# Conditioned attention on one core: scores before maxima in each step, the turn moved into a fill, and the last batch's rows loaded and biased one by one

## The chip, the cores and the metric

The kernel runs on one core of one Trainium2 chip. The metric is device time in microseconds (us) of one execution; three executions of the kernel before gave 1501.45, 1503.67 and 1509.83, median 1503.67.

## The reference, cut to what matters

Input x is [4, 1024, 512] (B batches, N tokens, D wide), 16 heads of 32. Everything is float32.

```python
h = _sln(x, w, ...)                      # layer norm, then gamma * ln + beta per batch
qkv = (h @ Wqkv.T + bqkv)                # q, k, v of 16 heads
energy = einsum('bhqd,bhkd->bhqk', q, k)
att = softmax(energy, axis=-1) / D ** 0.5
out = einsum('bhqk,bhkd->bhqd', att, v)
h1 = out @ Wp.T + bp + x
return _sln(h1, w, ...) + h1
```

There are 64 (batch, head) pairs. For each, the scores are a 1024 x 1024 matrix that is never stored: it is computed twice, once as A (rows are queries) to find each query's maximum, and once turned, as S^T (rows are keys), to be exponentiated and multiplied with v.

## The kernel before, in words

**Precision.** Projections split each float32 operand in a high and a low part and sum three products (`SPLIT`). A and S^T do the same in one matmul each, with parts stacked on partitions: A uses 96 rows (`a_item`, L737); S^T uses 98 rows (`turned_scores`, L751), the two more holding the negated maximum of each query in a high and a low part, so that S^T comes out with its maximum already subtracted.

**The clock of the program.** After a lead-in that projects five pairs of 128-token tiles, there are 16 iterations (i = 0 to 15) of four heads (s = 0 to 3), each head of eight steps (k = 0 to 7): step = 8 s + k. Each engine runs its own list of the same steps, and semaphores couple them. In every step TensorE (PE) does, in this order:

1. `project("start")`;
2. the first A block of the step (128 queries x 512 keys) into one of the two banks of `ps_a`;
3. the first S^T block of the next k (128 keys x 512 queries) into one of the three banks of `ps_st`;
4. `project("mid")`;
5. the second A block and, at k = 4, the turn (below);
6. the second S^T block;
7. in odd steps only, one set of pair sums (L781, 4 matmuls of 256 columns in four column groups, twice: softmax denominators) and 32 such matmuls in two calls of `weighted` (L768: v times the exponentials);
8. `project("end")`.

`project` takes a *fill*: a bank's worth of projection work. The table `PROJECTED` says which fill, which part and how many sixths of it run at which step and place. Fills 0 and 1 turn the normalised tiles (L691, four transposes each, at the start of steps 0 and 1); 2 to 5 are q and k (L702, matmuls of 256 columns); 6 and 7 are v and 8 and 9 the output projection (L649, matmuls of 512). Fills 0 to 7 belong to a later pair of tiles and are there in iterations 0 to 10 (`tiles`); 8 and 9 are there from iteration 4 on (`outs`). Every even step of iterations 4 to 9 has some 1.4 us of fill, half in the middle and half at the end (k = 2, 6) or all at the end (k = 0, 4). Iterations 11 to 14 have fills in steps 24 to 31 only; so in their first three heads the even steps hold nothing but A, S^T, A, S^T.

**Who releases whom.** VectorE (DVE) reduces each A block to a maximum per query (L1223, `half_max`); an A block may start when the reduction of the block two before it is done (`a_used`, two banks). A head's 16 blocks are spread so that the last is in step k = 3 of the head before; `max_negated` (L1240) then joins the halves. At k = 4, PE *turns* the 128 x 8 maxima into a row form: item 16, L731, a transpose that also takes a bank of `ps_a`, so that three items share that step's ring. DVE splits the result (`ring_row`, L1230 and L1232), SyncE (SP) copies it at k = 5 into rows 96 and 97 of `q_stack` (`store_row`, L435), and the next head's S^T, first needed at k = 7, waits for that copy (`row_in`).

ScalarE (ACT) exponentiates each S^T block (L999) into `p32`; an S^T block may start when the exponential of the block three before it is done. GpSimd (POOL) adds pairs of exponential slabs (`pair_add`, L1495) at k = 0, 2, 4, 6, and PE's pair sums wait for that: at k = 7 for the pair added at k = 4, and so on. POOL also has the layer norms (`norm_scale`, `norm_gain`, iterations 0 to 9), `residual`, `out_norm`, `out_low`, and the output's `out_scale` and `out_finish` (L1400 to L1414), which sit at steps 29, 31 and steps 1, 3 of the next iteration. `out_scale` at step 29 waits for statistics that DVE takes in step 28, behind `ring_row` on that engine.

**The last batch's rows.** The last batch's output is finished in another way: eight row tiles `acc[0..7]` hold x plus the bias `bp`, and the attention output is added to them at the end. `load_acc` (L480) on SP, after iteration 11's list, issues eight loads of 256 KB, all on one semaphore; `acc_add` (L1416) on POOL, also after iteration 11's list, waits for all eight and adds the bias to each (L1419). Their first reader is `pre_sum` in iteration 15. acc[0] to acc[3] lie in `x_tile` and `h_tile`, acc[4] to acc[7] in `qkT_s`, which are free once iteration 10 has projected its last tile.

Of the kernel before, what the change touches and what calls it, by code (L numbers as in the profile page):

```python
# [32 lines left out]
for _fill in range(3, 10):  # L33
    PROJECTED[4 * _fill - 8, "end"] = [(_fill, 0, 0, 6)]
    PROJECTED[4 * _fill - 6, "mid"] = [(_fill, 1, 0, 3)]
    PROJECTED[4 * _fill - 6, "end"] = [(_fill, 1, 3, 6)]
EVACUATED = {0: 0, 1: 1, 2: 3, 3: 7, 4: 11, 5: 15, 6: 19, 7: 23, 8: 27, 9: 31}
# [22 lines left out]
def conditioned_attention(nc, x, cond, ln_g, ln_b, Wg, bg, Wb, bb, Wqkv, bqkv, Wp, bp, out):  # L60
# [33 lines left out]
    with ExitStack() as ctx:  # L94
# [126 lines left out]
        acc_in = sem("acc_in")  # L221
# [29 lines left out]
        PRE_ADD_STEP = {17 + 2 * t: t for t in range(8)}  # L251
        LATE_MM_STEP = {8: 0, 10: 1}
# [100 lines left out]
        def _(sp):  # L353
# [126 lines left out]
            def load_acc():  # L480

                sp.wait_ge(tile_mm, 8 * PAIRS)
                for t in range(8):
                    T = 2 * END + t
                    sp.dma_start(acc[t], x_rows[T * 128:(T + 1) * 128, :]).then_inc(acc_in, 16)

# [65 lines left out]
            def iteration(i, tiles, norms, outs, first=False, last=False):  # L552
                pair = i - FIRST_OUTS
                for s in range(4):
                    u = 4 * i + s
                    for k in range(8):
# [34 lines left out]
                        if last and step == 5:  # L591

                            sp.wait_ge(out_pool, 10 * pair + ONE)
                            load_gain(go_s, go_in, pair)
                        if last and step in PRE_LOAD_STEP:
# [23 lines left out]
            iteration(LAST_TILES, False, False, True)  # L619
            load_acc()  # L620
# [21 lines left out]
        def _(pe):  # L642
# [193 lines left out]
            def iteration(i, tiles, outs, first=False, last=False):  # L836
                pair = i - FIRST_OUTS
                for s in range(4):
                    for k in range(8):
# [25 lines left out]
                        for use in uses[:1]:  # L865
                            a_item(*use)
# [3 lines left out]
                        if after:  # L870
                            turned_scores(*after, 0)
                        project("mid")
                        for use in uses[1:]:
                            a_item(*use)
                        if after:
                            turned_scores(*after, 1)
                        before = (i - (s == 0), (s - 1) % 4)
# [17 lines left out]
                        project("end")  # L895

# [435 lines left out]
        def _(pool):  # L1332
# [83 lines left out]
            def acc_add(t):  # L1416

                pool.wait_ge(acc_in, 128)
# [99 lines left out]
            def iteration(i, tiles, norms, outs, first=False, late=True):  # L1518
                pair = i - FIRST_OUTS
                ahead = i + LEAD  # L1520
                for step in range(32):
# [11 lines left out]
                    if norms and step in NORM_GAIN_STEP:  # L1533
                        norm_gain(ahead + 1, NORM_GAIN_STEP[step])
                    if outs and step in RESIDUAL_STEP:
# [19 lines left out]
            iteration(LAST_TILES, False, False, True)  # L1555
            for t in range(8):
                acc_add(t)
# [31 lines left out]
```

## Time and profile before

| | us |
|---|---|
| three executions | 1501.45, 1503.67, 1509.83 |
| median | 1503.67 |
| profiled execution, its own time | 1507.32 |
| its span | 1504.9 |
| PE busy | 1388.0 (92%) |
| POOL busy | 1004.3 (67%) |
| DVE busy | 916.5 (61%) |
| ACT busy | 715.4 (48%) |
| mean granted PE clock | 0.973 |

Engines are busy in the sense that an instruction of theirs is under way; successive matmuls overlap, so how fast PE goes is read from the distance between the starts of successive matmuls, not from its busy share. A wait stands in square brackets behind the instruction that ended it, with what released it.

### The profile page before, as it was taken

Reading aid. Unit: us, or ns where it says so; the run is one execution under the profiler, and the core shown is the slowest. Engines: PE = TensorE matmul, PEld = TensorE weight load, DVE = VectorE, ACT = ScalarE, POOL = GpSimd, SP = SyncE. Lnnn points to the kernel's source line nnn. Section 1 sums busy time; section 2 is a strip of 40 time slices with the busy share of each in tenths; the row PEclk is TensorE's granted clock in tenths of the full one; section 3 lists DMA queues with packets and bytes.
Section 4 is the critical chain, followed back from the end, with each engine's and each line's share of the span. In section 5 each row is a group of like instructions: output and inputs, shape, how many; then the busy total and the mean of one; then the engine's idle time right before and its main releaser. Section 6 shows DMA issues by size and latency. Waiting matters only on the chain.

```text
span 1504.9 us, 35271 instructions
## 1 busy us (share of the span) xinstructions
PE 1388.0 (92%) x10884; PEld 905.4 (60%) x10884; DVE 916.5 (61%) x1634; ACT 715.4 (48%) x1371; POOL 1004.3 (67%) x763
## 2 busy tenths in 40 slices
PE   6898999999999999999999999999996999998994
PEld 4887666666565657666666666666553454544562
DVE  5335766666666666666666666665663665665625
ACT  4221555555555555455454555455552545554441
POOL 2442455556465778687787878676877877787945
PEclk8899999999999999999999999999997998999997
DMA  7567533323334544445354534335333323243221
GB/s 226 154 188 207 135 88 109 98 88 98 103 99 120 135 110 130 99 140 135 105 146 121 147 101 130 97 114 137 87 103 106 106 82 101 77 116 95 67 65 59
DMA packets 216697, 174.01 MB, mean 116 GB/s; under 512 B 105492, under 2 KB 186516, under 8 KB 216632
## 3 DMA queue, kind: packets, MB, share of 16 engines
q1 hardware_dynamic: 214456, 166.83, 41.2%
q0 software_dynamic: 1984, 6.29, 1.1%
q8 instruction: 35, 0.57, 0.2%
q14 instruction: 30, 0.25, 0.1%
q10 hardware_dynamic: 192, 0.07, 0.0%
HBM read 113.29 MB, written 58.51 MB: 114 GB/s over the span
## 4 chain that ended last, share of the span: by engine, by line
PE 65%; POOL 14%; issue 9%; DVE 5%; POOLq 2%; DMA 1%; ACT 1%; SPq 1%; DVEq 0%; ACTq 0%
PE ps_a L737 13%; PE ps_st L751 11%; PE ps_o L768 11%; PE ps_w L702 8%; PE ps_w L649 7%; POOL p L1495 7%; PE ps_s L781 7%; DVE half_max L1223 3%; PE ps_st L702 3%; POOLq L1355 1%; POOL y_t L1412 1%; POOL y_t L1410 1%; PE ps_w L815 1%; PE ps_a L731 1%; PE ps_s L702 1%
## 5 line engine op out<-in xcount | busy, mean ns | idle before, releaser
L1223 DVE TENSOR_REDUCE half_max<-ps_a 128x1 f32<-128x512 f32 x1024 | 670.1, 687 | 455.8 <-PE ps_a L737 454.4
L999 ACT ACTIVATE p<-ps_st 128x512 f32<-128x512 f32 x1024 | 572.4, 597 | 490.2 <-PE ps_st L751 455.2
L1495 POOL TENSOR_TENSOR p<-p 128x1024 f32<-128x1024 f32 x248 | 590.7, 2384 | 300.1 <-PE ps_o L768 299.0
L737 PE MATMUL ps_a<-k_stack,q_stack 96*128 96x512 f32 x1024 | 449.4, 441 | 11.5 <-DVE half_max L1223 7.1
L751 PE MATMUL ps_st<-q_stack,k_stack 98*128 98x512 f32 x1024 | 415.1, 407 | 14.1 <-ACT p L999 14.1
L737 PEld LDWEIGHTS ps_a<-k_stack,q_stack 96*128 96x128 f32 x1024 | 193.9, 190 | 181.4 <-issue 99.1
L768 PE MATMUL ps_o<-p,v_head 128*32 128x256 f32 x4096 | 272.6, 384 | 0.0
L751 PEld LDWEIGHTS ps_st<-q_stack,k_stack 98*128 98x128 f32 x1024 | 195.4, 191 | 46.3 <-ACT p L999 25.2
L768 PEld LDWEIGHTS ps_o<-p,v_head 128*32 128x32 f32 x4096 | 134.4, 111 | 91.7 <-issue 6.3
L781 PE MATMUL ps_s<-p,root_s 128*32 128x256 f32 x1984 | 160.9, 397 | 20.1 <-POOL p L1495 18.5
L702 PEld LDWEIGHTS ps_w<-hT_s,wqkv_s 128*128 128x128 f32 x1056 | 143.7, 189 | 9.8
L702 PE MATMUL ps_w<-hT_s,wqkv_s 128*128 128x256 f32 x1056 | 146.6, 283 | 0.0
L781 PEld LDWEIGHTS ps_s<-p,root_s 128*32 128x32 f32 x1984 | 39.2, 108 | 110.5 <-issue 83.4
L649 PE MATMUL ps_w<-wqkv_s,hT_s 128*128 128x512 f32 x324 | 87.2, 395 | 0.0
L649 PE MATMUL ps_w<-wp_s,oT_s 128*128 128x512 f32 x288 | 78.3, 396 | 1.3 <-DVE h_t L1158 1.3
L649 PEld LDWEIGHTS ps_w<-wqkv_s,hT_s 128*128 128x128 f32 x324 | 60.9, 189 | 13.5
L649 PEld LDWEIGHTS ps_w<-wp_s,oT_s 128*128 128x128 f32 x288 | 53.7, 189 | 13.9 <-issue 1.7
L702 PE MATMUL ps_st<-hT_s,wqkv_s 128*128 128x256 f32 x360 | 49.9, 299 | 7.8 <-DVE hT_s L1122 7.8
L702 PEld LDWEIGHTS ps_st<-hT_s,wqkv_s 128*128 128x128 f32 x360 | 48.5, 205 | 9.6 <-DVE hT_s L1122 9.1
L1353 POOL TENSOR_TENSOR std_t<-mv_t,eps_s 128x1 f32<-128x1 f32 x32 | 6.0, 189 | 70.2 <-DVE mv_t L1082 70.2
L974 ACT ACTIVATE o_stage<-ps_o 128x256 f32<-128x256 f32 x63 | 24.2, 384 | 56.2 <-PE ps_o L768 56.2
L1373 POOL TENSOR_TENSOR h_tile<-h_tile,gq_s 128x512 f32<-128x512 f32 x32 | 41.1, 1283 | 14.7 <-DMA gq_s<-gain_bias_scratch 13.5
(167 smaller groups left out, 1003.8 us busy)
## 6 DMA issues: line engine op xcount, KB each, us to landing
qk_scratch<-qkT_s SPq DMA_DIRECT2D x108, 256.0 KB, 2.4
q_stack<-qk_scratch SPq DMA_DIRECT2D x192, 128.0 KB, 2.8
k_stack<-qk_scratch SPq DMA_DIRECT2D x192, 128.0 KB, 3.0
x_tile<-in_x SPq DMA_DIRECT2D x34, 256.0 KB, 5.1
gq_s<-gain_bias_scratch SPq DMA_DIRECT2D x16, 512.0 KB, 4.2
v_scratch<-v_parts SPq DMA_DIRECT2D x32, 256.0 KB, 3.3
v_head<-v_scratch SPq DMA_DIRECT2D x64, 128.0 KB, 2.1
att_scratch<-o_stage SPq DMA_DIRECT2D x240, 32.0 KB, 1.5
```

Of the source, the lines that this page charges most:

```text
L649: mm = pe.matmul(dst, left[:, lp, c, :], right[:, rp, c, :], start=(n == 0), stop=(n == 11))
L702: mm = pe.matmul(bank[:, part * 256:(part + 1) * 256], wqkv_s[:, lp, w, d, chunk * 128:(chunk + 1) * 128], hT_s[:, rp, d, :], start=(n == ...
L731: pe.transpose(ps_a[0:8, parity, 0:128], neg_max[:, s % 2, :], f_ident).then_inc(a_ready, 1)
L737: pe.matmul(ps_a[:, parity, :], q_stack[0:96, s, t * 128:(t + 1) * 128], k_stack[0:96, s, half * 512:(half + 1) * 512], start=True, stop=T ...
L751: pe.matmul(ps_st[:, ST_BANK[2 * k + e], :], k_stack[0:98, s, k * 128:(k + 1) * 128], q_stack[0:98, s, e * 512:(e + 1) * 512], start=True, ...
L768: mm = pe.matmul(ps_o[HD * e:HD * e + HD, 0:QW], v_head[:, s, k, :], p32[:, k, e * QW:(e + 1) * QW], start=(k == 0), stop=(k == 7))
L781: mm = pe.matmul(ps_s[HD * e:HD * e + HD, 0:QW], root_s[:], p32[:, 2 * j + 1, e * QW:(e + 1) * QW], start=(j == 0), stop=(j == 3))
L974: nc.scalar.activation(o_stage[:, s % 2, 0:QW], ps_o[:, 0:QW], ACT.Copy).then_inc(o_taken, 1)
L999: nc.scalar.activation(p32[:, k, e * 512:(e + 1) * 512], ps_st[:, ST_BANK[2 * k + e], :], ACT.Exp).then_inc(exp_done, 1)
L1223: V.tensor_reduce(half_max[:, s % 2, item:item + 1], ps_a[:, parity, :], AX.X, ALU.max).then_inc(a_used, 1)
L1373: G.tensor_tensor(h, h, gq_s[:, 0, :], ALU.mult).then_inc(ln_pool, 1)
L1495: G.tensor_tensor(p32[:, 2 * j + 1, :], p32[:, 2 * j, :], p32[:, 2 * j + 1, :], ALU.add).then_inc(pair_added, 1)
```

## The change

In each step PE issues S^T, A, S^T, A where it issued A, S^T, A, S^T. The place of `project("start")` and of the odd steps' sums and weighted products is the same.

The turn (the third item at k = 4) moves from between the second A and the second S^T to the end of the step. The fill parts that stood at the end of steps 4, 12, 20 and 28 are cut in two halves, and the turn is issued between the halves. In the last iteration it follows the second A directly.

`load_acc` and `acc_add` are issued one tile at a time inside iteration 11 (`gather=True`), at the steps of two new tables, with two semaphores for four tiles each in place of one for eight.

```diff
+for _step in (4, 12, 20, 28):
+    _fill = _step // 4 + 2
+    PROJECTED[_step, "end"] = [(_fill, 0, 0, 3)]
+    PROJECTED[_step, "last"] = [(_fill, 0, 3, 6)]
...
-        acc_in = sem("acc_in")
+        acc_in = [sem(f"acc_in{e}") for e in range(2)]
...
+        ACC_LOAD_STEP = {2: 0, 3: 1, 5: 2, 6: 3, 12: 4, 15: 5, 16: 6, 18: 7}
+        ACC_ADD_STEP = {9: 0, 10: 1, 11: 2, 13: 3, 22: 4, 24: 5, 25: 6, 27: 7}
...
-            def load_acc():
-
-                sp.wait_ge(tile_mm, 8 * PAIRS)
-                for t in range(8):
-                    T = 2 * END + t
-                    sp.dma_start(acc[t], x_rows[T * 128:(T + 1) * 128, :]).then_inc(acc_in, 16)
+            def load_acc(t):
+
+                if t == 0:
+                    sp.wait_ge(tile_mm, 8 * PAIRS)
+                T = 2 * END + t
+                sp.dma_start(acc[t], x_rows[T * 128:(T + 1) * 128, :]).then_inc(acc_in[t // 4], 16)
...
+                        if gather and step in ACC_LOAD_STEP:
+                            load_acc(ACC_LOAD_STEP[step])
...
-            iteration(LAST_TILES, False, False, True)
-            load_acc()
+            iteration(LAST_TILES, False, False, True, gather=True)
...
                         project("start")
-                        for use in uses[:1]:
-                            a_item(*use)
                         after = (i, s, k + 1) if k < 7 else (i + (s + 1) // 4, (s + 1) % 4, 0)
                         if last and (s, k) == (3, 7):
                             after = None
                         if after:
                             turned_scores(*after, 0)
+                        for use in uses[:1]:
+                            a_item(*use)
                         project("mid")
-                        for use in uses[1:]:
-                            a_item(*use)
                         if after:
                             turned_scores(*after, 1)
+                        for use in uses[1:2]:
+                            a_item(*use)
+                        if last:
+                            for use in uses[2:]:
+                                a_item(*use)
...
                         project("end")
+                        if not last:
+                            for use in uses[2:]:
+                                a_item(*use)
+                        project("last")
...
-                pool.wait_ge(acc_in, 128)
+                pool.wait_ge(acc_in[t // 4], 64)
                 G.tensor_tensor(acc[t], acc[t], bp_s[:], ALU.add).then_inc(acc_ready, 1)
...
+                    if gather and step in ACC_ADD_STEP:
+                        acc_add(ACC_ADD_STEP[step])
...
-            iteration(LAST_TILES, False, False, True)
-            for t in range(8):
-                acc_add(t)
+            iteration(LAST_TILES, False, False, True, gather=True)
```

## Rows read from the trace of the kernel before

**Rows 1.** The page, part 4: the chain that ended last, by engine

```profile
PE 65%; POOL 14%; issue 9%; DVE 5%; POOLq 2%; DMA 1%; ACT 1%; SPq 1%; DVEq 0%; ACTq 0%
```

**Rows 2.** Five iterations: length; busy us of PE, PEld, DVE, ACT, POOL; clock; DMA; GB/s

```profile
644.10:728.80 84.70, 81.99 (x670) 55.25 (x670) 55.20 (x100) 43.73 (x85) 65.95 (x51) 1.00 0.46 124
...
1065.70:1137.20 71.50, 67.74 (x542) 36.81 (x541) 47.42 (x84) 39.37 (x74) 57.73 (x39) 1.00 0.36 99
1137.20:1225.00 87.80, 71.47 (x542) 38.36 (x541) 47.51 (x84) 39.31 (x74) 67.20 (x47) 0.88 0.36 100
1225.00:1301.70 76.70, 71.42 (x541) 38.53 (x540) 47.50 (x84) 39.36 (x74) 57.38 (x39) 0.93 0.34 90
1301.70:1373.90 72.20, 67.68 (x541) 36.80 (x540) 47.38 (x84) 39.43 (x74) 57.51 (x39) 1.00 0.35 96
```

**Rows 3.** Timeline of PE: an even step with fill, no turn

```profile
707.57 0.50 PE L737 MATMUL ps_a<-k_stack,q_stack 96*128 96x512 f32 x1
...
710.02 0.39 PE L737 MATMUL ps_a<-k_stack,q_stack 96*128 96x512 f32 x1
```

**Rows 4.** Timeline of PE: step 28 of i = 6, fill and turn

```profile
717.38 0.50 PE L737 MATMUL ps_a<-k_stack,q_stack 96*128 96x512 f32 x1
...
718.74 0.27 PE L731 MATMUL ps_a<-ident,neg_max 128*8 128x128 f32 x1 [0.41 <-DVE half_max L1223]
...
719.19 1.55 PE L649 MATMUL ps_w<-wp_s,oT_s 128*128 128x512 f32 x6
720.59 0.39 PE L737 MATMUL ps_a<-k_stack,q_stack 96*128 96x512 f32 x1
```

**Rows 5.** Timeline of PE: a turn in i = 10, which is no loop

```profile
995.41 0.27 PE L731 MATMUL ps_a<-ident,neg_max 128*8 128x128 f32 x1 [0.31 <-DVE half_max L1223]
995.44 0.48 PE L751 MATMUL ps_st<-q_stack,k_stack 98*128 98x512 f32 x1
```

**Rows 6.** Timeline of PE: steps 0 and 1 of i = 7

```profile
728.04 0.65 PE L691 MATMUL ps_w<-ident,h_tile 128*128 128x128 f32 x4
...
729.86 0.50 PE L751 MATMUL ps_st<-q_stack,k_stack 98*128 98x512 f32 x1 [0.49 <-ACT p L999]
...
732.28 0.50 PE L751 MATMUL ps_st<-q_stack,k_stack 98*128 98x512 f32 x1 [0.44 <-ACT p L999]
732.71 0.64 PE L781 MATMUL ps_s<-p,root_s 128*32 128x256 f32 x8
```

**Rows 7.** Timeline of ACT, the same steps

```profile
729.22 1.08 ACT L999 ACTIVATE p<-ps_st 128x512 f32<-128x512 f32 x2
```

**Rows 8.** Timeline of DVE, the end of step 31 and step 0

```profile
727.12 0.68 DVE L1158 TENSOR_TENSOR h_t<-ps_w,res_t 128x512 f32<-128x512 f32 x1
...
729.71 0.68 DVE L1122 TENSOR_TENSOR hT_s<-ps_w,hT_s 128x512 fp32r<-128x512 f32 x1
```

**Rows 9.** Timeline of PE: an even and an odd step of i = 11, no fill

```profile
1095.97 0.50 PE L737 MATMUL ps_a<-k_stack,q_stack 96*128 96x512 f32 x1
...
1097.26 0.49 PE L737 MATMUL ps_a<-k_stack,q_stack 96*128 96x512 f32 x1
...
1098.52 0.64 PE L781 MATMUL ps_s<-p,root_s 128*32 128x256 f32 x8
```

**Rows 10.** Timeline of SP: the row copies of that head

```profile
1093.79 1.43 SPq L435 DMA_DIRECT2D q_stack<-max_rows  x2
```

**Rows 11.** Timelines of POOL and PE: the last batch's rows

```profile
1145.65 2.47 POOL L1419 TENSOR_TENSOR x_tile<-x_tile,bp_s 128x512 f32<-128x512 f32 x2 [6.42 <-DMA qkT_s<-in_x]
...
1157.78 1.08 PE L781 MATMUL ps_s<-p,root_s 128*32 128x256 f32 x8 [13.65 <-POOL p L1495]
```

**Rows 12.** PE waits for POOL at step 7 of i = 13, 14; then a stretch

```profile
1242.89 1.08 PE L781 MATMUL ps_s<-p,root_s 128*32 128x256 f32 x8 [2.24 <-POOL p L1495]
...
1318.74 0.64 PE L781 MATMUL ps_s<-p,root_s 128*32 128x256 f32 x8 [1.50 <-POOL p L1495]
...
1243.00:1255.00 12.00, 11.91 (x72) 5.83 (x76) 5.48 (x9) 5.67 (x11) 6.88 (x3) 0.63 0.21 50
```

More of the change, by code:

```diff
@@ L550, in _, with iteration @@
                 store_v(LEAD - 1, a)
-            def iteration(i, tiles, norms, outs, first=False, last=False):
+            def iteration(i, tiles, norms, outs, first=False, last=False, gather=False):
                 pair = i - FIRST_OUTS
@@ L1516, in finish_late, with iteration @@
                     out_finish(pair, 1, count)
-            def iteration(i, tiles, norms, outs, first=False, late=True):
+            def iteration(i, tiles, norms, outs, first=False, late=True, gather=False):
                 pair = i - FIRST_OUTS
```

## The prediction

> **What bounds the kernel now.** I read the chain first, then the iterations one by one, then the timelines of PE inside a step. The chain [rows 1] is PE for 65% and POOL for 14%, so PE's pace decides except where POOL holds it. The iterations [rows 2] say where: i = 6, with all its fills, takes 84.7 us; i = 11 and i = 14, with few, take 71.5 and 72.2; i = 12, with the work of i = 14, takes 87.8, and i = 13 takes 76.7. Both of these have a granted clock under 1. In a full iteration PE's starts follow each other with hardly a hole; what is lost there are small waits that come back in each iteration, and these a new order can touch. A half per cent (7.5 us) is about what a measurement of this kernel can tell from no change.
>
> **1. The last batch's rows.** POOL stands 6.42 us for the eight loads and then has eight additions of about 1.25 us (2.47 for two) in one piece; PE waits 13.65 us for a pair sum behind them and then runs at the low clock for a while [rows 11]. With the additions spread, i = 12 has the same lists as i = 14 on every engine. I take its length: 87.8 - 72.2 = 15.6 us gained; by i = 13 it would be 11.1 [rows 2]. The additions, 10 us, go into i = 11, where POOL is idle for 71.5 - 57.7 = 13.8 us [rows 2]; a pair addition may be some 4 us late before PE's sums ask for it, and no step gets more than one of 1.25 us. So I cost them at nothing; without that cover it would be at most 10. On SP the eight loads are issued between its other transfers, two at most in neighbouring steps of 1.3 to 2.7 us; a transfer holds SP's queue for some 0.7 us (1.43 for two, [rows 10]), and behind them wait stack loads for a head three ahead. The first addition is at step 9, three steps after the fourth load. Nothing.
>
> **2. The turn.** An even step with six fill matmuls and no turn takes 710.02 - 707.57 = 2.45 us from its first A to the next [rows 3]; with a turn 720.59 - 717.38 = 3.21 [rows 4]. So a turn costs 0.76 us, and 0.41 of that is a wait: it is the third item in a ring of two, and the reduction of the step's first A is not done. After three fill matmuls (half of the 1.4 us between 719.19 and 720.59) that reduction is done with about 0.2 us to spare, and the bank is handed back before the second A of the next step. What remains of the cost is the turn itself and perhaps a weight load behind it that nothing hides. From below it is 0.03, the distance from a turn to the next matmul in [rows 5]; from above, 0.35, all of the 0.76 but the wait. I take 0.15, near the low end, since the distance is of the same instruction and the rest of the 0.76 is what follows a stall. Gain 0.6 in a loop; in i = 0 and 10, which are no loops, the wait is 0.31 [rows 5] and I take 0.45. Turns with a fill that PE's own pace bounds: 3 in each of i = 0 to 3, 4 in i = 4 to 9, 3 in i = 10: 39, of which 6 in i = 0 and 10. 33 x 0.6 + 6 x 0.45 = 22.5 us.
>
> The rows show weight loads of 0.19 us hidden in a stream whose matmuls start every 0.23 us. The Trainium skill (TensorE: Matmul & The Clock Gate, "The mechanism" in Part 3) says that a weight load overlaps running matmuls only where its row group differs. By that rule the turn and the fill behind it would each pay their load, and the saving would be nearer 0.4 a turn, some 15 us in all. The stream of loads over the same rows speaks against it here; I stay with 22.5.
>
> **3. The new order where fills are.** Exchanging A with S^T changes no count, and the waits it could touch are few. In steps 0 and 1 of i = 0 to 10 it costs. The second S^T of step 0 starts at 729.86 because an exponential ends there that had to follow the copy of the fill turned at 728.04 [rows 6, 7]; the new order doesn't move that, but one A (0.33 behind a stall) now comes after it in place of before. In step 0 most of this is hidden, since the next transposes wait for VectorE's subtraction that ends at 730.4 [rows 8]; that one is 0.1 later, as the first A is. In step 1 the sums at 732.71 [rows 6] come 0.34 later. 11 x 0.34 = +3.7 us. In step 31, VectorE's sum of h1 [rows 8] follows the second reduction, which is 0.23 later, and the transposes of step 0 follow it: +0.2 at six starts of iterations, +1.2.
>
> **4. The new order where no fill is.** From the first A to the sums of the next step: 1098.52 - 1095.97 = 2.55 us, with the third A at 1.29, when the first one's reduction is done [rows 9]. Now S^T goes first (0.34), the third A is at 0.34 + 1.19 = 1.53, the fourth, by two reductions of 0.65, at 2.14, and the sums at 2.47 to 2.57. So each of some 45 such pairs of steps gains 0.08 or loses 0.02; 12 of the turns there are where the turn has no fill to stand in, worth up to 0.1 each to the bad. I take -1 for all, bounds -3.6 and +2. The row copy is later relative to its reader here: it is issued at 1093.79 for 1.43 us [rows 10], and the reader comes some 2.3 us after that ends; the change takes 0.7 of it. Nothing, but little is left: a copy that lands 1 us late would be waited for.
>
> **5. POOL at the start of iterations.** From step 29 to step 7 POOL is behind: PE waits 2.24 and 1.50 us at step 7 of i = 13 and 14 [rows 12]. This run of work begins with statistics that VectorE takes behind the turn, and the turn of step 28 is now 0.36 later in its step. So at the five starts of i = 11 to 15 the turn's saving (not counted above) is lost and 0.36 added: +1.8 us. PE's wait there grows by 0.9. After 2.24 us of it the clock was 0.63 over 12 us, so about 9 us at the low of its levels, 1.2 in place of 2.4 GHz, 4.5 us lost; after 1.50 it was not [rows 12, 2]. With waits of 2 to 3 us, i = 11, 12 and 14 can fall too. I put this at +3.5, between 0 and three times 4.5.
>
> **The sum.** -15.6 - 22.5 + 3.7 + 1.2 - 1 + 1.8 + 3.5 = -28.9 us. The profiled execution took 1507.3 (span 1504.9) and would take 1478.4. It stands 3.6 above the median of the runs; from the median, 1503.7, it is **1474.8 us**.
>
> **The rivals.**
> - *Only the rows gain (chance 0.09).* PE gets ahead by each turn and hands it back in a wait for ScalarE or POOL. For: the waits of 0.49 and 0.44 [rows 6] show that S^T can be held. Against: in a full iteration POOL is busy 66 of 84.7 us and ScalarE 44 [rows 2]. Time: 1503.7 - 15.6 = 1488.
> - *The clock falls at every start without fills (0.05).* i = 11, 12, 14 and 15 each lose 4.5 as i = 13 does: 1474.8 - 3.5 + 18 = 1489.
> - *The stall of i = 12 moves into i = 11 (0.03).* Its POOL is late at steps 9 to 13 or 22 to 27 by the whole 10 us, and PE waits for it: 1485.
> - *A dearer border (0.03, slower).* In every odd step S^T now follows the weighted products and the sums follow A; no row shows either. S^T after A starts at 0.23, but behind a drained array at 0.34. If each of the two borders in 256 odd steps costs that difference of 0.11, it is 56 us: 1531. From 0.056 a border (29 us) it decides. Against: both loads take 0.19, and A and S^T follow fills alike.
> - *Nothing changes (0.01)*: the turn still waits in its new place, and a wait elsewhere takes the rest.
>
> **The numbers.** The forecast has 0.79. Its own bounds: turns at 0.8 of their saving or 1.1, clock from 0 to 9, rows 11.1 or 15.6, no-fill steps from -3.6 to +2: about 1465 to 1486. For 8 in 10 with the other cases I take 1464 to 1491. Faster by over 0.5% (under 1496.2) 0.94, within 0.03, slower 0.03.
>
> **What would show it.** Right: no wait of PE before the turn in iterations 0 to 10, and a full iteration of about 83 us in place of 84.7 (4 x 0.6 less 0.34 and 0.2); i = 12 between 72 and 77; POOL's L1419 in eight single pieces with no wait for loads; the wait before the sums of step 7 longer than 2 us in i = 13. Wrong: a full iteration of 84.7, with new waits of L751 for ACT; turns that still wait for DVE; L1419 followed by a wait of L781 in i = 11; distances over 0.34 at the borders of odd steps.

## The result and the profile after

The changed kernel takes 1481.96 us (median of 4, 1479.04 to 1484.65) against 1502.82 (median of 4, 1501.45 to 1509.83). The ratio is 0.9852, with a 95% interval of 0.9815 to 0.9888: 20.9 us less, where 28.9 were forecast; it lies inside the range. The two profiled executions stand 28.3 us apart (1507.32 and 1479.04), close to the forecast, but that is luck: the one before is among the longer of its kernel, the one after is the shortest of its own. What differs between executions of one kernel comes up below.

The chain that ended last has moved little against [rows 1]: PE has 67% of it where it had 65%, DVE 3% where it had 5%.

```profile
PE 67%; POOL 14%; issue 9%; DVE 3%; POOLq 2%; DMA 2%; ACT 1%; SPq 1%; ACTq 0%; DVEq 0%
```

By iterations, with the columns of [rows 2]: i = 6, 8, 11, 12, 13 and 14.

```profile
634.90:718.90 84.00, 82.33 (x670) 55.57 (x669) 55.49 (x100) 43.10 (x84) 65.90 (x51) 0.98 0.47 125
801.40:883.90 82.50, 80.82 (x672) 55.22 (x670) 55.53 (x100) 43.00 (x84) 65.87 (x51) 1.00 0.48 129
1049.50:1122.50 73.00, 67.54 (x545) 37.61 (x541) 47.42 (x84) 38.64 (x74) 67.03 (x47) 1.00 0.46 124
1122.50:1196.90 74.40, 69.12 (x544) 38.36 (x540) 47.39 (x84) 38.79 (x74) 57.47 (x39) 0.98 0.35 92
1196.90:1271.20 74.30, 68.97 (x544) 38.53 (x540) 47.50 (x84) 38.88 (x74) 57.46 (x39) 0.98 0.35 93
1271.20:1344.20 73.00, 67.54 (x545) 37.66 (x541) 47.43 (x84) 38.76 (x74) 57.48 (x39) 1.00 0.35 95
```

A full iteration such as i = 8 went from 84.6 to 82.5. Iteration 12 went from 87.8 to 74.4, but 11 and 14, at 73.0, are longer than before (71.5 and 72.2). And i = 6 has 1.5 us more than i = 8 with the same work, at a clock of 0.98: that is new against the trace of the kernel before, where all iterations up to 11 had a clock of 1.00 (traces of other kernels in the old order have some too, as counted below).

The turn of step 28 of i = 6 (timeline of PE), which answers to [rows 4]:

```profile
708.27 0.50 PE L758 MATMUL ps_st<-q_stack,k_stack 98*128 98x512 f32 x1
...
709.31 0.87 PE L656 MATMUL ps_w<-wp_s,oT_s 128*128 128x512 f32 x3
710.02 0.27 PE L738 MATMUL ps_a<-ident,neg_max 128*8 128x128 f32 x1
710.04 0.94 PE L656 MATMUL ps_w<-wp_s,oT_s 128*128 128x512 f32 x3
710.83 0.40 PE L758 MATMUL ps_st<-q_stack,k_stack 98*128 98x512 f32 x1
```

It waits for nothing, and the step takes 710.83 - 708.27 = 2.56 us, 0.11 more than the 2.45 of the same step without a turn [rows 3] and 0.65 less than before. The weight loads of the same place (timeline of PEld) lie over running matmuls: the turn's own, 0.08 us, begins at 709.87, and the next one of the fill at 710.02.

```profile
709.87 0.08 PEld L738 LDWEIGHTS ps_a<-ident,neg_max 128*8 128x8 f32 x1
710.02 0.53 PEld L656 LDWEIGHTS ps_w<-wp_s,oT_s 128*128 128x128 f32 x3
```

The start of i = 8, steps 0 and 1, which answers to [rows 6]:

```profile
801.00 0.65 PE L698 MATMUL ps_w<-ident,h_tile 128*128 128x128 f32 x4 [0.27 <-DVE h_t L1172]
...
802.83 0.50 PE L758 MATMUL ps_st<-q_stack,k_stack 98*128 98x512 f32 x1 [0.70 <-ACT p L1013]
803.16 0.39 PE L744 MATMUL ps_a<-k_stack,q_stack 96*128 96x512 f32 x1
...
805.34 0.51 PE L758 MATMUL ps_st<-q_stack,k_stack 98*128 98x512 f32 x1 [0.71 <-ACT p L1013]
805.68 0.40 PE L744 MATMUL ps_a<-k_stack,q_stack 96*128 96x512 f32 x1
806.01 0.64 PE L788 MATMUL ps_s<-p,root_s 128*32 128x256 f32 x8
```

From the transposes to the sums it is 5.01 us where it was 4.67: the waits of S^T for ACT are 0.70 and 0.71 where they were 0.49 and 0.44, with an A behind each, and the transposes now wait 0.27 for the sum of h1.

The last batch's rows (timeline of POOL, i = 11) are biased in single pieces with no wait for their loads; PE's wait of 13.65 us [rows 11] is gone.

```profile
1072.20 1.27 POOL L1433 TENSOR_TENSOR x_tile<-x_tile,bp_s 128x512 f32<-128x512 f32 x1
1073.44 2.38 POOL L1509 TENSOR_TENSOR p<-p 128x1024 f32<-128x1024 f32 x1
```

At step 7 of i = 12, PE waits 2.24 us for POOL and goes on at the low clock; L775 takes 1.95 where it takes 1.05 at full clock. The same wait is 1.86 in i = 11, 2.25 in i = 13 and 2.26 in i = 14; after those of i = 11 and 14 the clock stayed at 1.00. The lines of i = 12:

```profile
1140.71 0.85 PE L788 MATMUL ps_s<-p,root_s 128*32 128x256 f32 x8 [2.24 <-POOL p L1509]
1141.32 1.95 PE L775 MATMUL ps_o<-p,v_head 128*32 128x256 f32 x16
```

### The profile page after: what moved, and what is told of

Read it like the earlier page. It is cut to its first block, busy times and chain, and to the rows that moved or that the text cites. A ratio compares the mean times of both kernels' runs of the same rounds, so it can differ in the third digit from the quotient of the medians.

```text
span 1476.4 us, 35271 instructions
## 1 busy us (share of the span) xinstructions
PE 1376.7 (93%) x10884; PEld 910.2 (62%) x10884; DVE 920.9 (62%) x1634; ACT 706.4 (48%) x1371; POOL 1004.0 (68%) x763
## 4 chain that ended last, share of the span: by engine, by line
PE 67%; POOL 14%; issue 9%; DVE 3%; POOLq 2%; DMA 2%; ACT 1%; SPq 1%; ACTq 0%; DVEq 0%
PE ps_st L758 14%; PE ps_a L744 12%; PE ps_o L775 11%; PE ps_w L709 9%; POOL p L1509 8%; PE ps_w L656 8%; PE ps_s L788 7%; PE ps_st L709 3%; DVE half_max L1237 2%; POOLq L1369 1%; POOL y_t L1426 1%; POOL y_t L1424 1%; PE ps_w L822 1%; ACT p L1013 1%; PE ps_w L698 1%
## 5 line engine op out<-in xcount | busy, mean ns | idle before, releaser
L1013 ACT ACTIVATE p<-ps_st 128x512 f32<-128x512 f32 x1024 | 565.4, 597 | 419.4 <-PE ps_st L758 392.7
L758 PE MATMUL ps_st<-q_stack,k_stack 98*128 98x512 f32 x1024 | 439.4, 431 | 22.4 <-ACT p L1013 22.0
L744 PE MATMUL ps_a<-k_stack,q_stack 96*128 96x512 f32 x1024 | 421.2, 413 | 12.7 <-DVE half_max L1237 8.5
L775 PE MATMUL ps_o<-p,v_head 128*32 128x256 f32 x4096 | 272.7, 385 | 0.0
L775 PEld LDWEIGHTS ps_o<-p,v_head 128*32 128x32 f32 x4096 | 134.3, 111 | 91.2 <-issue 4.6
L788 PE MATMUL ps_s<-p,root_s 128*32 128x256 f32 x1984 | 160.5, 395 | 11.4 <-POOL p L1509 9.7
L709 PE MATMUL ps_w<-hT_s,wqkv_s 128*128 128x256 f32 x1056 | 149.9, 286 | 0.0
```

Of the source, the lines that this page charges most:

```text
L709: mm = pe.matmul(bank[:, part * 256:(part + 1) * 256], wqkv_s[:, lp, w, d, chunk * 128:(chunk + 1) * 128], hT_s[:, rp, d, :], start=(n == ...
L744: pe.matmul(ps_a[:, parity, :], q_stack[0:96, s, t * 128:(t + 1) * 128], k_stack[0:96, s, half * 512:(half + 1) * 512], start=True, stop=T ...
L758: pe.matmul(ps_st[:, ST_BANK[2 * k + e], :], k_stack[0:98, s, k * 128:(k + 1) * 128], q_stack[0:98, s, e * 512:(e + 1) * 512], start=True, ...
L775: mm = pe.matmul(ps_o[HD * e:HD * e + HD, 0:QW], v_head[:, s, k, :], p32[:, k, e * QW:(e + 1) * QW], start=(k == 0), stop=(k == 7))
L788: mm = pe.matmul(ps_s[HD * e:HD * e + HD, 0:QW], root_s[:], p32[:, 2 * j + 1, e * QW:(e + 1) * QW], start=(j == 0), stop=(j == 3))
L1013: nc.scalar.activation(p32[:, k, e * 512:(e + 1) * 512], ps_st[:, ST_BANK[2 * k + e], :], ACT.Exp).then_inc(exp_done, 1)
```

## The experiments

The theory was the sum of the prediction with its parts independent: rows, turn, order, POOL's start, clock. The main rival was that the order belongs to the turn's gain. The question that the result added was what the missing 8 us were. The kernel before was measured again beside each group of runs, and its medians there lie between 1502.8 and 1505.3; so medians of different groups compare to some 2.5 us only, and the ratios, each to the kernel before beside it, are the safer figures.

### The parts one by one

**e1: rows alone.** Edit, on the kernel before: the hunks of `load_acc`, `acc_add` and their tables, nothing else.

```diff
-            iteration(LAST_TILES, False, False, True)
-            for t in range(8):
-                acc_add(t)
+            iteration(LAST_TILES, False, False, True, gather=True)
```

> The kernel before with only the last batch's rows loaded and biased one by one in iteration 11. Theory (the three parts add up; the rows part is worth what iteration 12 lost): iteration 12 falls from 87.8 us to 72 to 77, iteration 11 stays at 71.5, and the time is 1487 to 1491 against 1503. Rival (additions in iteration 11 delay POOL, as the wait at step 5 of iteration 11 in the changed kernel might say): iteration 11 is longer by 1 us or more here too, and the time is over 1492.

Measured: 1491.35 us, ratio 0.9916 (0.9897 to 0.9935), 11.9 less than the 1503.22 of the kernel before beside it. Iterations 11, 12 and 13:

```profile
1056.20:1130.60 74.40, 69.06 (x541) 37.20 (x540) 47.45 (x84) 39.27 (x74) 67.53 (x47) 0.98 0.43 122
1130.60:1202.80 72.20, 67.74 (x541) 36.86 (x541) 47.41 (x84) 39.42 (x74) 57.67 (x39) 1.00 0.34 96
1202.80:1276.20 73.40, 68.95 (x541) 37.66 (x541) 47.46 (x84) 39.51 (x74) 57.58 (x39) 0.98 0.35 94
```

Iteration 12 has the 72.2 us that it was to have, 15.6 less. But i = 11 has 2.9 more at a clock of 0.98. PE at steps 5 and 7 of i = 11 (timeline of PE), where the kernel before had a single wait of 1.11 at step 7 and no low clock after it:

```profile
1077.31 0.64 PE L784 MATMUL ps_s<-p,root_s 128*32 128x256 f32 x8 [0.80 <-POOL p L1498]
...
1083.25 1.08 PE L784 MATMUL ps_s<-p,root_s 128*32 128x256 f32 x8 [1.89 <-POOL p L1498]
```

POOL's additions begin only at step 9, so it isn't they that hold POOL. It is late from its start: its third instruction of the output's scale for the second tile comes after a gap of 1.86 us that no other engine ends, where the kernel before has 0.24. The timeline of POOL at that place, before and then e1:

```profile
1070.79 0.57 POOL L1356 TENSOR_TENSOR ostd_t<-ostd_t,minus_half 128x1 f32<-128x1 f32 x1 [0.24 <-issue]
```

```profile
1072.02 0.57 POOL L1359 TENSOR_TENSOR ostd_t<-ostd_t,minus_half 128x1 f32<-128x1 f32 x1 [1.86 <-issue]
```

The traces say what ends the gap: the landing of the output tile that POOL stored itself a little earlier. In the program a `pool.drain()` stands just before this instruction (`power`, L1355 in the kernel before). In e1 the store is issued at 1066.83 and takes 5.0 us to land, so it is there at 1071.84, and the instruction starts at 1072.02; before, it was issued at 1067.22 and took 2.9, so that it had landed at 1070.11 and nothing was left to wait for. The stores, before and then e1 (timeline of POOL, and the list of the DMAs issued at that moment, with their size and the us to landing):

```profile
1067.22 0.63 POOL L1414 DMA_DIRECT2D out_y<-y_t  x1 [0.29 <-POOL y_t L1412]
out_y<-y_t POOLq DMA_DIRECT2D x1, 256.0 KB, 2.9
```

```profile
1066.83 0.63 POOL L1417 DMA_DIRECT2D out_y<-y_t  x1 [0.29 <-POOL y_t L1415]
x_tile<-in_x SPq DMA_DIRECT2D x2, 256.0 KB, 4.9
out_y<-y_t POOLq DMA_DIRECT2D x1, 256.0 KB, 5.0
```

In all fourteen traces, wherever POOL stands over 0.3 us at this place (111 times), it goes on 0.18 us after its last store has landed, and nowhere does it go on sooner. In i = 11 the gap is 0.8 to 1.9 us in every trace with the row loads there (the changed kernel, e1, e4 to e8, e11, e12) but that of e9, whose POOL issues its store of the first tile earlier and has 0.24. Without the loads it is 0.24 (before, e2, e3) or 0.57 (e10). But the row loads aren't needed for it: in every trace but e9's it is 1.7 to 3.9 us in i = 5 to 9 and 1.0 to 2.0 in i = 15, and in i = 13 of the kernel before it is 1.18. That the row loads make the store of i = 11 land late is argued from this comparison; no run moved them alone.

So both theories had a part, and the time is 0.4 past the range of the first: the wait of i = 12 went, and the work moved into i = 11 isn't free there. 15.6 less in i = 12 and 2.9 more in i = 11 make 12.7, within the interval of the 11.9. The other differences of these two traces (1.5 more in i = 6, 3.3 less in i = 13) hold low clock that falls otherwise in each execution. The profiled execution of the kernel before was one of its longer ones; the one of e1 is near its median.

**e2: order alone.** S^T, A, S^T, A; the turn third, behind the second A; no fill cut.

```diff
-                        for use in uses[:1]:
-                            a_item(*use)
                         if after:
                             turned_scores(*after, 0)
+                        for use in uses[:1]:
+                            a_item(*use)
                         project("mid")
-                        for use in uses[1:]:
-                            a_item(*use)
                         if after:
                             turned_scores(*after, 1)
+                        for use in uses[1:]:
+                            a_item(*use)
```

> The kernel before with only S^T, A, S^T, A in each step; the turn stays the third item, behind the second A, with no fill cut. Theory (the order by itself only costs: 0.33 in steps 0 and 1 of eleven iterations, 0.23 in step 31 of six, 0.5 at step 20 of four, and stretches of low clock that begin at these waits): 1503 + 4 + 1.4 + 2 + 0 to 5 = 1510 to 1516. Rival (the order is what lets the turn go without a wait, so it gains with it): the turn's step is shorter here than 3.21 us by 0.2 or more, and the time is at most 1503.

Measured: 1515.88 us, ratio 1.007 (1.0053 to 1.0087), 12.7 more and inside the expected range. The order by itself only costs. Its turn waits as before, and the step is no shorter (3.30 us here, 3.21 in [rows 4]):

```profile
725.98 0.27 PE L731 MATMUL ps_a<-ident,neg_max 128*8 128x128 f32 x1 [0.41 <-DVE half_max L1223]
```

**e3: turn alone.** The turn between the halves of the end fill, order A, S^T, A, S^T.

```diff
-                        for use in uses[1:]:
+                        for use in uses[1:2] if not last else uses[1:]:
                             a_item(*use)
...
                         project("end")
+                        if not last:
+                            for use in uses[2:]:
+                                a_item(*use)
+                        project("last")
```

> The kernel before with only the turn moved into the middle of the end fills; order A, S^T, A, S^T kept. Theory (the turn's saving of 0.67 us in a loop and 0.49 outside needs no new order): 39 turns save 25 us, less 1 to 2 us at the starts of iterations 11 to 15: 1479 to 1482. Rival (part of the saving comes with the new order, which puts a matmul more between the first A and the turn): the turn still waits, and the time is over 1487.

Measured: 1484.01 us, ratio 0.9865 (0.9846 to 0.9884), 19.2 less. The turn waits for nothing and costs the same 0.1 us as in the changed kernel, so its gain needs no new order:

```profile
703.84 0.87 PE L653 MATMUL ps_w<-wp_s,oT_s 128*128 128x512 f32 x3
704.54 0.27 PE L735 MATMUL ps_a<-ident,neg_max 128*8 128x128 f32 x1
704.57 0.94 PE L653 MATMUL ps_w<-wp_s,oT_s 128*128 128x512 f32 x3
```

The 19.2 is 2 us past the end of what was expected: 39 turns are worth 25, and 6, not 1 to 2, are given back later (e7 and e8). Its trace says the same: 24.8 less than before in iterations 0 to 10, 5.5 more behind them.

**e4: turn and rows, the old order.** The changed kernel with the body of a step as in e3.

> The changed kernel with the old order A, S^T, A, S^T (turn inside the fill and rows one by one kept). Theory (the new order costs 3.6 + 1.4 us of waits at the starts of iterations, 2 us at step 20, and up to 5 us of low clock): 1470 to 1475, faster than the changed kernel's 1482 by 7 to 12, and no stretch at the low clock in iterations 1 to 10. Rival (the order is neutral and the stretches of low clock come by chance): 1479 to 1484, with such stretches here too.

Measured: 1470.57 us, ratio 0.978 (0.9757 to 0.9802): 11.4 less than the changed kernel's 1481.96 (the two intervals don't meet), and no stretch of low clock in iterations 1 to 10. The parts add up: 19.2 + 11.9 = 31.1 against 32.7 for both together, and the order takes 11.4 to 12.7 of that back. It does so in the early iterations: 1 to 10 take 817.9 and 816.1 us in the two traces of the changed kernel and 808.0 in e4, 11 to 14 take 294.7 and 299.5 against 298.6.

### What the order costs

**e5: the old order in steps 0 and 1 of iterations 0 to 10 only.**

```diff
+                        early = tiles and step < 2
+                        if early:
+                            for use in uses[:1]:
+                                a_item(*use)
                         if after:
                             turned_scores(*after, 0)
-                        for use in uses[:1]:
-                            a_item(*use)
+                        if not early:
+                            for use in uses[:1]:
+                                a_item(*use)
```

(and the same around the second pair).

> The changed kernel with the order A, S^T, A, S^T in steps 0 and 1 of iterations 0 to 10 alone. Theory (there the second S^T waits for an exponential behind the copy of a turned fill, and an A placed after it costs 0.33 us an iteration and leaves PE idle long enough for the clock to fall now and then): iterations 1 to 10 each 0.33 us shorter, no stretch at the low clock in them, 3.6 us less and up to 5 more: 1475 to 1479. Rival (the stretches are chance): 1478.5, and such stretches stay.

Measured: 1475.03 us, ratio 0.9802 (0.9786 to 0.9819): 6.9 less than the changed kernel, from twenty-two of its 512 steps (7.6 less than e6 below, which was measured beside it and takes what the changed kernel takes). A full iteration takes 82.1 where the changed kernel's i = 8 takes 82.5:

```profile
795.40:877.50 82.10, 80.79 (x669) 55.33 (x668) 55.28 (x100) 43.00 (x84) 65.78 (x50) 1.00 0.49 130
```

The waits themselves are 11 x 0.34 = 3.7 us of it. The rest fits the clock: no low stretch here in iterations 1 to 10, and by the count under e11 the new order has some 1.9 more of them in an execution, at 1.5 us each: 2.8.

**e6: ScalarE's copies one step later in iterations 11 to 14.** In these, step 21 had become longer, 3.33 us where it had been 2.66.

```diff
-                    highs = LATE_HIGH_STEP if last else OUT_HIGH_STEP
+                    highs = LATE_HIGH_STEP if last else OUT_HIGH_STEP if tiles else {20: 0, 22: 1}
```

> The changed kernel with ScalarE's two copies for the output projection (steps 19 and 21) one step later in iterations 11 to 14. Theory (S^T of step 20 waits there for an exponential behind such a copy, which itself waits for POOL's multiplication of step 18): steps 20 to 22 of iterations 11 to 14 shorter by 0.5 each, 2 us in all: 1480. Rival (the waits at steps 20 to 22 come from the ring of A and its reductions): no change, 1482, steps 21 still 3.3 us.

Measured: 1482.58 us, ratio 0.9848 (0.9827 to 0.9869). PE in i = 12 of the changed kernel, from S^T of step 20 that waits for ACT to the first S^T of steps 21 and 22:

```profile
1169.27 0.51 PE L758 MATMUL ps_st<-q_stack,k_stack 98*128 98x512 f32 x1 [0.38 <-ACT p L1013]
...
1169.89 0.49 PE L758 MATMUL ps_st<-q_stack,k_stack 98*128 98x512 f32 x1
...
1173.22 0.50 PE L758 MATMUL ps_st<-q_stack,k_stack 98*128 98x512 f32 x1
```

And with the copies later:

```profile
1174.31 0.49 PE L758 MATMUL ps_st<-q_stack,k_stack 98*128 98x512 f32 x1
...
1177.13 0.50 PE L758 MATMUL ps_st<-q_stack,k_stack 98*128 98x512 f32 x1
```

Step 21 is 2.82 in place of 3.33, so the wait was of these copies, and it is of the new order's making, which asks for that S^T 0.23 us earlier. The total is unchanged: the 2 us don't show beside low stretches that fell otherwise. As a gain this is not shown.

**e11: the changed kernel once more, for its trace.** No edit.

> The changed kernel unaltered, for one more trace. Theory (the new order's longer waits in steps 0 and 1 let the clock fall now and then): one to four stretches of about 3.3 us at the low clock at the starts of iterations 1 to 10, not at the same iterations as before, and all other step lengths the same to 0.03 us. Rival (they are of the program, not of chance): the same three places.

Measured: 1482.75 us (one run). Low stretches at the starts of i = 4 and 8, at 474 and 805 us; in the first trace they were at 393, 640 and 970. In iterations 11 to 14 the clock fell after the wait at step 7 in all four, where in the first trace it fell in 12 and 13 alone. The step lengths are the same elsewhere. This is how one looks, i = 6 of the first trace, step 1:

```profile
638.85 0.50 PE L758 MATMUL ps_st<-q_stack,k_stack 98*128 98x512 f32 x1 [0.70 <-ACT p L1013]
639.19 0.56 PE L744 MATMUL ps_a<-k_stack,q_stack 96*128 96x512 f32 x1
639.68 1.08 PE L788 MATMUL ps_s<-p,root_s 128*32 128x256 f32 x8
640.54 1.93 PE L775 MATMUL ps_o<-p,v_head 128*32 128x256 f32 x16
```

I counted such stretches (matmuls at twice their spacing for over 2 us) in iterations 1 to 10 of every trace. With the new order in steps 0 and 1 (the changed kernel twice, e2, e6): 9 in 40 iterations. With the old order there (the kernel before, e1, e3, e4, e5, e7 to e10, e12): 4 in 100. So they are tied to no iteration, and come some five times as often where PE stands 0.70 and 0.71 us in steps 0 and 1 as where it stands 0.49 and 0.44; a split as uneven as 9 and 4 would come once in some 600 times if the stretches fell on any iteration alike. A stretch of 3.2 us costs 1.5, as i = 6 beside i = 8 shows.

### POOL's start

**e7: the statistics of step 28 taken in step 27**, on e4.

```diff
-OUT_STATS_STEP = {28: 0, 31: 1}
+OUT_STATS_STEP = {27: 0, 31: 1}
```

> The faster version (turn inside the fill and rows one by one, old order) with VectorE's output statistics of step 28 taken in step 27, ahead of the turn's split. Theory (POOL's run of work at the starts of iterations 11 to 15 begins with these statistics, and PE's wait of 2.25 us at step 7 hangs on its start): PE's waits there fall to about 1 us and the clock stays up: iterations 11 to 14 at 71 to 73 us in place of 74.2 to 75.2, time 1462 to 1467 against 1470.6. Rival (POOL is late for another reason, the amount of its work between the steps): waits stay over 2 us, 1469 to 1472.

Measured: 1459.99 us, ratio 0.9694 (0.9678 to 0.9711): 10.6 less than e4 and 2 below the expected range (13 less if the ratios are compared). PE's wait at step 7 of i = 13, e4 first, then e7:

```profile
1203.97 0.64 PE L788 MATMUL ps_s<-p,root_s 128*32 128x256 f32 x8 [2.25 <-POOL p L1506]
```

```profile
1201.76 0.64 PE L788 MATMUL ps_s<-p,root_s 128*32 128x256 f32 x8 [1.22 <-POOL p L1506]
```

In i = 14 the same wait went from 2.27 to 1.25. Iteration 14 in e4 and in e7:

```profile
1260.80:1335.90 75.10, 70.24 (x544) 38.19 (x540) 47.51 (x84) 38.96 (x74) 57.46 (x39) 0.95 0.32 93
```

```profile
1256.20:1327.80 71.60, 67.80 (x545) 36.71 (x541) 47.37 (x84) 38.99 (x74) 57.56 (x39) 1.00 0.35 97
```

One microsecond less of wait and a clock of 1.00 in place of 0.95: 3.5 us in one iteration. The largest wait of this kind is at step 5 of i = 15, where ScalarE stands for POOL and PE for ScalarE: PE's was 3.52 us before the change, 4.84 in the changed kernel, 4.75 in e4, and is 2.77 here.

**e8: the turn of step 28 in its old place, in iterations 11 to 14 only**, on e4.

```diff
+                        soon = last or (step == 28 and not tiles)
-                        for use in uses[1:2] if not last else uses[1:]:
+                        for use in uses[1:] if soon else uses[1:2]:
                             a_item(*use)
...
-                        if not last:
+                        if not soon:
```

> The same faster version with the turn of step 28 of iterations 11 to 14 back in its old place between the second A and the second S^T. Theory (moving that turn gave POOL a start 0.36 us later and PE 0.67 us less, so it only lengthened PE's wait at step 7, past the length at which the clock falls): PE's wait falls from 2.25 to about 1.2 to 1.5 us, iterations 12 to 15 lose 0.3 to 2.5 us each, time 1463 to 1470. Rival (the turn saves its 0.67 us there as elsewhere): 4 x 0.67 us more, 1473.

Measured: 1465.37 us, ratio 0.9732 (0.9716 to 0.9748): 5.2 less than e4 (7 by the ratios) for undoing four of the turns. The wait at step 7 of i = 14 is

```profile
1278.30 0.64 PE L788 MATMUL ps_s<-p,root_s 128*32 128x256 f32 x8 [1.50 <-POOL p L1507]
```

that is, what it was before the change [rows 12]. Moving a turn to save PE 0.67 us cost 1.3 us net here, through POOL and the clock.

**e9: also `out_scale` at step 27 and `out_finish` at 29**, on e7.

```diff
-OUT_SCALE_STEP = {29: 0}
-OUT_FINISH_STEP = {31: 0}
+OUT_SCALE_STEP = {27: 0}
+OUT_FINISH_STEP = {29: 0}
```

> The faster version with the statistics in step 27, and also POOL's out_scale at step 27 in place of 29 and out_finish at 29 in place of 31. Theory (POOL's run of work at the starts of iterations 11 to 15 only starts too late; before step 29 POOL has some 6 us idle): PE's waits at step 7, 1.2 to 1.9 us with the statistics moved alone, go, and the time is 1453 to 1458 against 1460. Rival (the run is bound by its amount from step 31 on, where out_scale of the second tile still waits): waits of over 1 us stay, 1459 to 1461.

Measured: 1462.24 us, ratio 0.9709 (0.9687 to 0.9732): nothing gained over e7's 1459.99; the 2 us more are within the intervals. The waits at step 7 of i = 12 to 14 are 1.50 and 1.77, longer than e7's 0.89 to 1.25.

The edit doesn't do what the theory asks for. At the start of i = 13, POOL's scale of the first tile comes 1.2 us earlier than in e7, after a wait of 3.70 for the statistics; but a pair addition that went ahead of it in e7 comes behind it, and the scale of the second tile, which decides, begins 1.15 us later. So e9 says nothing against a late start. In i = 13 of the traces in the old order, PE's wait goes with the lateness of that second scale and the gap behind the store (both of POOL):

| | second scale, us after the start of i = 13 | gap | PE's wait at step 7 |
|---|---|---|---|
| e7 | 4.10 | 0.67 | 1.22 |
| e8 | 4.79 | 0.24 | 1.44 |
| e12 | 4.10 | 1.30 | 1.81 |
| e9 | 5.25 | 0.24 | 1.77 |
| e4 | 5.85 | 0.24 | 2.25 |

Each wait is the sum of the first two columns less 3.6 to 3.8 us. e7 and e12 start at the same moment there, and PE's wait differs by the 0.6 us by which the gap does. So a part of what e7 leaves is POOL standing for its own store; the rest, POOL's work from step 29 on, is argued.

**e10: the same statistics in step 27 in the kernel before.**

> The kernel before with the statistics of step 28 taken in step 27, nothing else. Theory (POOL's late start binds there too, by the waits of 1.1 to 2.2 us at step 7, but without the turn's saving it binds less): 3 to 8 us less than before, 1495 to 1500. Rival (before the change these waits were too short to matter and only the moved turn made them count): within 2 us of before, 1501 to 1505.

Measured: 1505.59 us, ratio 1.0002 (0.9989 to 1.0015): no change. Full iterations are 85.2 where they were 84.6 (the statistics hold DVE when the first A of step 28 comes, and the turn, still third in its ring, waits for that too), and i = 14 is 71.6:

```profile
733.10:818.40 85.30, 81.90 (x672) 55.21 (x670) 55.12 (x100) 43.65 (x84) 65.97 (x50) 1.00 0.47 124
1304.30:1375.90 71.60, 67.71 (x544) 36.79 (x540) 47.25 (x84) 39.37 (x74) 57.46 (x39) 1.00 0.37 97
```

The time is the rival's, 0.8 from the kernel before beside it, but not for the rival's reason: the waits at step 7 were there and went, from 1.11, 2.24 and 1.50 in i = 11, 13 and 14 to 0.25, 0.80 and 0.28. Six full iterations that are 0.6 longer, 3.6 us, took it back.

**e12: the statistics in step 27 only from iteration 10 on**, on e4.

```diff
+                        when = OUT_STATS_STEP if norms else {27: 0, 31: 1}
-                        if outs and step in OUT_STATS_STEP and not last:
-                            a = OUT_STATS_STEP[step]
+                        if outs and step in when and not last:
+                            a = when[step]
```

> The faster version with the statistics in step 27 only from iteration 10 on, and in step 28 in iterations 4 to 9 as in the kernel before. Theory (taken earlier, they hold VectorE when the first A of step 28 comes, and so cost PE 0.3 us in each full iteration, where POOL has time to spare; they gain only at the starts of iterations 11 to 15): iterations 4 to 9 back at 81.9 us, iterations 11 to 14 at 71 to 72, time 1457 to 1459. Rival (what is gained there is lost again in stretches of low clock): 1460 to 1462.

Measured: 1457.75 us, ratio 0.9686 (0.967 to 0.9702), the lowest median: 24.2 less than the changed kernel, 45.7 less than the kernel before beside it. It isn't told apart from e7's ratio of 0.9694, whose interval overlaps; that iterations 4 to 9 are back at 81.9 is what the trace shows. Iterations 8 and 14:

```profile
794.30:876.20 81.90, 80.81 (x672) 55.23 (x669) 55.31 (x100) 43.27 (x84) 65.89 (x51) 1.00 0.48 130
...
1254.80:1326.30 71.50, 67.70 (x544) 36.69 (x540) 47.32 (x84) 38.96 (x74) 57.54 (x39) 1.00 0.35 97
```

## Why the prediction was right, and where it was off

It was right that the kernel gets faster, by two of three parts, and that the new order is no gain. That the time came within 8 us owes something to terms that err against each other. The rows gave 3.7 less than forecast and the order cost 7.5 to 8.8 more; turn and POOL's start together gave 2.0 more than forecast (e3: 19.2 against 22.5 - 5.3), and the parts together 1.6 more than singly. That leaves 7.6 to 8.9 of the missing 8. By its own steps:

- **The rows, step 1: right in place, too large in size.** The 15.6 of i = 12 came in full, yet the rows alone gave -11.9 (e1). That POOL's additions cost nothing held: POOL is busy 67.0 of 73.0 us of i = 11, no addition waits and nothing waits for one. The term that failed is the nothing at which the loads were put: with them beside it POOL stands 0.8 to 1.9 us in place of 0.24 for the landing of its own store, PE waits longer behind it, and i = 11 takes 2.9 us more in e1. That the loads delay the store is argued from which traces have it; no run moved the loads alone.
- **The turn, step 2: right.** 0.11 us left of 0.76 where 0.15 was taken; 33 x 0.65 and 6 x 0.49 make 24.4 where the sum had 22.5. The rule of the Trainium skill (TensorE: Matmul & The Clock Gate, "The mechanism" in Part 3) that a weight load overlaps running matmuls only where its row group differs, by which a turn would have saved some 0.4, is not borne out: the turn's 0.02 to the next matmul and 0.08 more for the three after it leave no room for two weight loads of 0.08 and 0.19 laid end to end.
- **The order where fills are, step 3: the sizes right, a consequence missed.** 0.34 a start was forecast for steps 0 and 1 and 0.34 came, 0.2 for h1 and 0.23 came. What the step didn't price is that longer waits there make the clock fall: 9 in 40 starts against 4 in 100. Together with steps 20 to 22 it is this that failed: steps 3 and 4 summed to +3.9 and the order costs 11.4 to 12.7 (e2, e4). e5 puts 6.9 of that in steps 0 and 1 alone. With 1.4 for h1 and the 2.0 at steps 20 to 22, whose removal in e6 gained nothing, 10.3 of it has a name.
- **The order where no fill is, step 4: no gain.** An even and an odd step take 1.05 + 2.93 = 3.98 us in the changed kernel, measured from S^T, and took 1.29 + 2.70 = 3.99. The reasoning about the ring was right and its bound of 0 was the answer, not -1. The hold of S^T by ACT at step 20 was not seen; it is 0.5 us in each of four iterations. The row copies, of which it said that little was left, were waited for once in i = 11 of each trace in the new order and in no trace's other iterations: 0.35 and 0.18 us in the changed kernel, 0.57 in e2, 0.71 in e6 (up to 0.27 in e4, e5 and e9).
- **POOL's start, step 5: the mechanism right, the price low.** The wait grew by some 0.8 where 0.9 was forecast (1.1 to 1.9 at i = 11, 1.50 to 2.3 at i = 14), and e8 shows the turn of step 28 to be its cause. At i = 13 it stayed, 2.25 after 2.24, since the rows alone had brought it down to 1.53 (e1): the 2.24 from which the prediction reckoned was of the stall in i = 12. So the sign "longer than 2 us in i = 13" could not tell the two apart. With the clock the step was put at +5.3 for five starts, and four of them cost 5.2 to 7 (e8). The 10.6 of e7 isn't the price of this step: it holds lateness that was there before. A low stretch of the changed kernel cost some 1.5 us and not the 4.5 of i = 13 before, and came at more starts.
- **The step from the profiled execution to the median** was sound in itself, but the row terms were taken from one execution, whose low stretches are of its own. The kernel before had some 10 us of low clock in i = 13 and none before i = 12 in that trace.

Of the rivals, none came true as a whole. "The clock falls at every start without fills" was the nearest in mechanism (in e11 it did fall in i = 11 to 14, but for some 1.5 us lost each time in place of 4.5); "a dearer border" is excluded but for a trace of it: S^T after the weighted products starts 0.98 after them, as A did, and only where the last A had waited do the sums follow at 0.43 in place of 0.33.

Left open: whether SP's row loads are what makes POOL's store land late in i = 11; a run with the loads some steps later would tell. Also 1.1 to 2.4 us of what the order costs. And what sets the chance that the clock falls at a wait of a given length. A wait of 1.09 us was followed by a low stretch (e8, i = 12) and one of 2.26 was not (i = 14 of the changed kernel's first trace).

## What to carry to other kernels

Split a change into its parts before believing its sum: here two parts of three were worth 33 us and the third, which none of them needed, gave 12 back. An item that waits in a short ring is best moved behind work that was due anyway, and then checked for who was counting on its old time: a turn that comes later in its step held the statistics behind it, those held POOL, and POOL held PE. Where an engine stands behind a store of its own and the profile names no releaser, compare the end of the wait with the landing of the store, as with POOL here. When engines are this close together, price a wait by its length and by what the clock does after it.

## What was not expected of the hardware

PE's clock fell after waits far shorter than the 13.65 and 2.24 us of the trace before. Two waits of 0.7 us in steps 0 and 1 were followed by 3.2 us at the low level in 9 of 40 cases, at other iterations in the two traces of the changed kernel. This is a part of what makes executions of one kernel differ: of fifteen executions of the kernel before, the shortest, 1501.39 us, had a mean granted clock of 0.977 and the longest, 1508.97, one of 0.972. It makes a single profiled execution a poor base for a difference of 8. POOL stood up to 3.9 us at a `drain` for a store that it had issued itself, and went on 0.18 us after the landing each time, though the profile names no releaser for it. And the same edit (e7, e10) was worth 10.6 us in one version and nothing in another, by what else was on the edge there.
